# A rewoven order behind convolution 2, and x2 copied as whole rows of 66

## The chip, the core and the metric

The kernel runs on one core of a Trainium2 chip. The metric is device time in microseconds (us), the median of repeated executions; lower is better.

## The reference

Eight images of 64 x 64 pixels and 48 channels, float32, NHWC, go through four layers in a row:

```python
# L0: channel attention (q, k, v from a 48x144 product, gram of q and k over the 4096 pixels),
#     then 1x1 conv 96->96, leaky ReLU, 3x3 conv 96->96, leaky ReLU, 1x1 conv 96->48, plus x
# L1: 3x3 depthwise conv, 1x1 conv 48->48, batch norm, after a ReLU
# L2: router = sigmoid(mean over pixels @ Wr + br), 4 experts;
#     1x1 expand 48->192 (mixed weights), ReLU, 3x3 depthwise (mixed), ReLU, 1x1 48<-192, plus its input
# L3: as L1, other weights
```

Each image's layer 2 needs the mean of layer 1's whole output, and each image's convolution in layer 0 needs sums over all of its pixels; these are the two points at which an image can't go on by chunks.

## The kernel before

Every engine has its instructions written out by hand: one function `iteration(f, attn, back)` for each, with the same meaning of its three images. While image f is in convolution 2, layer 1 and the start of layer 2, image attn = f + 1 is in the attention of layer 0, and image back = f - 1 is in the end of layer 2 and layer 3. Iteration 0 and 7 stand apart (no back, no attn); 1 to 6 are a loop. The rest of image 7 follows behind the loop.

An image is handled in chunks of 512 pixels (one PSUM bank, `BANK`): 8 chunks for layer 0 and the expansion (`CHUNKS`), and, with even and odd rows on separate partitions (0 to 47, and 64 to 111), 4 chunks in layers 1 and 3 and in the projection (`PCHUNKS`). PSUM's eight banks are four rings of two (`Ring`); `take` makes PE wait until the reader of the entry two before is done.

PE (line 1261): conv2, 8 chunks of 24 matmuls, then w3 (96->48); l1 and l3 are `pair_conv` (1154 ff.), 15 matmuls a chunk, 5 of them on `b_parts`, shifted copies that SyncE makes by six DMAs a chunk (`copy_beside`, 876 and 880), once the high and low parts of this chunk and the next are there. transpose_x, attention_scores, attention_sums (1078), attention_gather and attention_weights are the attention of attn; project (1230 ff.) and out_tokens (1245) belong to back; routing, expand_halo and expand (1181 f.) to f. conv1 weaves q transposes (1105), conv1's matmuls (1113) and the expansions.

ScalarE (line 1472): it takes PSUM out: x_out (1330), scores_out, two squares a group (1340), l1_out (1434 with an accumulator, then 1438), project_affine (1425, 1426), l3_out (1448), tokens_out (1461), the sigmoid of route (1443) and the square roots; first_tap and finish_unit (1386) belong to the depthwise units.

VectorE (line 794): the depthwise taps (659, 1024 elements a partition each; `steps_at` says how many stand in which place, the last four numbers after convolution 2), low parts (`l1_low_part`, `l3_low_part`, line 738: v minus its high part; `x2_low_part`, 751), mean_out (756, 758), norms_begin (594 to 602: it waits for all 16 squares of attn, releases `u_ready` at 596, and goes on to the norms of q), mix_weights (767 to 791), norms_end (609 to 612), the sums' copies (620 to 624), conv1_weights (629 to 633), and the h1b rows of the expansion (667, 675).

GpSimd: scale_k (997) after `u_ready`, which PE's attention_sums waits for, and the low parts of conv1's output.

SyncE's queue, in this order: load of x, `beside_l1` (4 times `copy_beside`), `beside_l3` (4 times), `copy_x2` (903), the store of back (912), `copy_thirds`. The layer 1 result is written as x2_h and x2_l into rows 33 to 64 of `y1_parts`, columns 1 to 64 of 66; copy_x2 brings it to `x2`, where expansion and project read it: four DMAs, each 48 partitions of 32 rows of 64 numbers, once project of back is done with the old x2.

## Time and profile before

| | |
|---|---|
| median of 3 runs | 1163.04 us (1160.52 to 1165.03) |
| the profiled execution | 1161.86 us, its span 1160.0 us |
| PE busy | 1049.4 us, 4808 matmuls |
| VectorE busy | 858.6 us |
| ScalarE busy | 470.9 us |
| GpSimd busy | 90.4 us |
| granted TensorE clock, mean | 0.963 |

The profile is of one execution. The busy times of engines overlap. A busy PE is one whose matmuls are in flight; a clock of 1.00 is 2.4 GHz, 0.50 is 1.2 GHz. In the timeline a row merges neighbouring instructions of one line; the brackets behind it give the idle time of the engine ahead of it and what released it.

### The profile page before, as it was taken

To read this page: it belongs to the slowest core of one execution; us is meant where nothing else is said; L and a number is where in the kernel's file an instruction comes from. 1 tells how busy PE (TensorE), PEld (TensorE's weight loads), DVE (VectorE), ACT (ScalarE), POOL (GpSimd) and SP (SyncE) were. 2 spreads that over 40 slices of the span, in tenths; PEclk is the share of its full clock that TensorE was granted. 3 is DMA by queue.
4 is the path that set the end of the run, shared out by engine and by line. 5 is a ranking of instruction groups with operands and counts; after the bars stand their busy time and mean duration, and the time that the engine had idled before them with its cause. 6 is when DMAs were issued, how large, how long until landed. Compare 5 with 4: busy or idle time off the path is not lost.

```text
span 1160.0 us, 14937 instructions
## 1 busy us (share of the span) xinstructions
PE 1049.4 (90%) x4808; PEld 667.8 (58%) x4808; DVE 858.6 (74%) x1193; ACT 470.9 (41%) x812; POOL 90.4 (8%) x72
## 2 busy tenths in 40 slices
PE   4699789998999999999999999999999999977986
PEld 3465566556665666556665666557565666535534
DVE  6742569976798669976899659976799669972870
ACT  3311533354533643354533633354523643334331
POOL 0300011000200011000200011000200011000000
PEclk9889979999999999999999989999999999989998
DMA  4224325236423545236523535236423551236114
GB/s 67 60 53 73 73 39 88 48 77 127 91 32 72 112 85 87 45 76 125 101 33 80 109 73 87 45 72 124 94 34 79 111 87 43 47 71 131 21 24 97
DMA packets 169904, 86.79 MB, mean 75 GB/s; under 512 B 145455, under 2 KB 146324, under 8 KB 169876
## 3 DMA queue, kind: packets, MB, share of 16 engines
q1 hardware_dynamic: 169876, 86.44, 40.1%
q8 instruction: 15, 0.25, 0.1%
q14 instruction: 13, 0.11, 0.0%
HBM read 10.82 MB, written 6.29 MB: 15 GB/s over the span
## 4 chain that ended last, share of the span: by engine, by line
PE 63%; DVE 13%; issue 9%; SPq 6%; ACT 4%; DMA 4%; POOL 0%; DVEq 0%; ACTq 0%; POOLq 0%
PE bank L1132 12%; PE bank L1137 12%; PE bank L1143 8%; DVE dwa L659 6%; PE bank L1166 5%; PE bank L1113 4%; PE bank L1234 4%; DMA x_odd<-y_parts 3%; PE bank L1154 3%; PE bank L1181 3%; SPq L903 2%; PE bank L1182 2%; PE bank L1105 2%; SPq L876 2%; PE bank L1169 2%
## 5 line engine op out<-in xcount | busy, mean ns | idle before, releaser
L659 DVE SCALAR_TENSOR_TENSOR dwa<-h1a,dyn,dwa 128x1024 f32<-128x1024 f32 x240 | 293.2, 1276 | 0.0
L659 DVE SCALAR_TENSOR_TENSOR dwb<-h1b,dyn,dwb 128x1024 f32<-128x1024 f32 x128 | 155.9, 1275 | 0.0
L1132 PE MATMUL bank<-y_parts,w_l 96*96 96x512 f32 x576 | 152.1, 409 | 0.0
L1137 PE MATMUL bank<-y_parts,w_h 128*96 128x512 f32 x576 | 148.7, 402 | 0.0
L1166 PE MATMUL bank<-a_parts,wt_h 128*112 128x512 f32 x384 | 118.2, 416 | 11.8 <-ACT dwa L1448 7.7
L1132 PEld LDWEIGHTS bank<-y_parts,w_l 96*96 96x96 f32 x576 | 91.7, 163 | 61.0 <-issue 21.3
L1137 PEld LDWEIGHTS bank<-y_parts,w_h 128*96 128x96 f32 x576 | 93.8, 163 | 44.6
L1166 PEld LDWEIGHTS bank<-a_parts,wt_h 128*112 128x112 f32 x384 | 64.1, 177 | 46.0 <-issue 16.9
L1003 POOL TENSOR_TENSOR y_parts<-y,y_parts 96x512 fp32r<-96x512 f32 x56 | 67.1, 1199 | 203.6 <-DVE y L699 203.5
L1398 ACT ACTIVATE y<-bank,b2s 96x512 f32<-96x512 f32 x32 | 21.9, 683 | 141.2 <-PE bank L1143 141.2
L1143 PE MATMUL bank<-y_parts,w_one 128*96 128x512 f32 x192 | 76.6, 399 | 0.0
L1143 PE MATMUL bank<-y_parts,w_two 128*96 128x512 f32 x192 | 76.2, 397 | 0.0
L738 DVE SCALAR_TENSOR_TENSOR a_parts<-v,a_parts 112x512 fp32r<-112x512 f32 x64 | 43.5, 689 | 43.2 <-ACT a_parts L1426 40.4
L997 POOL TENSOR_TENSOR tok<-tok,u 128x1536 f32<-128x1536 f32 x8 | 22.4, 2796 | 667.2 <-DVE u L596 667.2
L1113 PE MATMUL bank<-xq,w_cur 97*96 97x512 f32 x128 | 66.8, 603 | 3.5 <-DVE y L699 3.5
L1398 ACT ACTIVATE xq<-bank,b2s 96x512 f32<-96x512 f32 x32 | 21.9, 685 | 117.0 <-PE bank L1143 108.4
L698 DVE TENSOR_TENSOR y_parts<-bank,y 96x512 fp32r<-96x512 f32 x64 | 44.0, 687 | 22.8 <-ACT y L1370 22.7
L1448 ACT ACTIVATE dwa<-bank,conv_bias,inv 112x512 f32<-112x512 f32 x32 | 24.9, 778 | 83.5 <-PE bank L1169 83.5
L1166 PE MATMUL bank<-a_parts,wt_l 128*112 128x512 f32 x192 | 57.0, 405 | 0.0
L1068 PE MATMUL bank<-qkw,xcm 113*128 113x192 f32 x256 | 49.6, 337 | 7.1 <-ACT tok L1340 5.3
L1363 ACT ACTIVATE xq<-bank 96x512 f32<-96x512 f32 x64 | 37.5, 586 | 41.6 <-PE bank L1105 41.6
L1168 PE MATMUL bank<-y_parts,wt_h 128*112 128x512 f32 x128 | 51.3, 401 | 0.0
(246 smaller groups left out, 1706.9 us busy)
## 6 DMA issues: line engine op xcount, KB each, us to landing
y_parts<-a_parts SPq DMA_DIRECT2D x64, 198.0 KB, 3.0
y_parts<-a_parts SPq DMA_DIRECT2D x64, 197.6 KB, 3.4
tok<-in_x_dram SPq DMA_DIRECT2D x48, 192.0 KB, 4.8
a_parts<-a_parts SPq DMA_DIRECT2D x128, 66.0 KB, 2.4
y_parts<-y_parts SPq DMA_DIRECT2D x64, 131.9 KB, 2.3
x_even<-y_parts SPq DMA_DIRECT2D x16, 384.0 KB, 7.5
x_odd<-y_parts SPq DMA_DIRECT2D x16, 384.0 KB, 9.9
out_dram<-dwb SPq DMA_DIRECT2D x32, 192.0 KB, 4.1
```

What stands on the lines that cost most here:

```text
L659: nc.vector.scalar_tensor_tensor(out=dst, in0=tap_input(n, t), scalar=weight, in1=dst, op0=ALU.mult, op1=ALU.add).then_inc(tap_step, 1)
L698: nc.vector.tensor_tensor(y1_view(y1_h, k - 1), bank.rearrange("p (j w) -> p j w", w=W), y1_tokens(k - 1), ALU.max).then_inc(y1h_ready, 1)
L1003: nc.gpsimd.tensor_tensor(y1_view(y1_l, k), y1_tokens(k), y1_view(y1_h, k).bitcast(F32), ALU.subtract).then_inc(y1l_ready, 1)
L1068: last = nc.tensor.matmul(bank[:, m * 2 * C2:(m + 1) * 2 * C2], xcm[:, i * 128:(i + 1) * 128], qkw[:, :], start=True, stop=True)
L1113: nc.tensor.matmul(bank[0:C2, :], w1_cur[:, :], xq[:, (k - 1) % 2, :], start=True, stop=True)\
L1132: nc.tensor.matmul(bank[0:C2, :], w2_l[:, t, :], y1_h[:, rows, cols], start=t == 0, stop=False)
L1137: nc.tensor.matmul(bank[0:C2, :], w2_h[:, t, :], y1_parts[:, 0, rows, cols], start=False, stop=False)
L1143: last = nc.tensor.matmul(bank[0:C2, :], wgt[:, kh, :], y1_parts[:, 1, rows, cols], start=False, stop=kh == 2 and kw == 2)
L1166: nc.tensor.matmul(bank[0:P2, :], wgt[layer][:, kw, :], own[:, rows, kw:kw + W], start=n + kw == 0, stop=False)
L1168: nc.tensor.matmul(bank[0:P2, :], wgt[layer][:, 3, :], beside[:, rows, 1:W + 1], start=False, stop=False)
L1234: last = nc.tensor.matmul(bank[par * ODD_AT:par * ODD_AT + C, :], pc[:, part, :], src[:, :, par, :], start=False, stop=n == 1)
L1398: nc.scalar.activation(y2[(k // 2) % 2][:, (k % 2) * BANK:(k % 2 + 1) * BANK], ring_c.bank(C_2 + k)[0:C2, :], ACT.Identity, bias=b2s[:, 0: ...
```

## The change

PE's order behind convolution 2 becomes: l1(0), w3(3), x transposes, project(0, 1), l1(1), transposes, scores 0 to 3, l1(2), scores 4 to 7, project(2), l1(3), project(3), routing, l3(0), half of the attention sums, l3(1), out_tokens(0), the other half, l3(2), out_tokens(1), gather, l3(3), weights, out_tokens(2), halo, out_tokens(3), expand 0 and 1, and conv1. ScalarE's and VectorE's orders follow it: norms_begin is cut in two, its first part (to `u_ready`) goes between x2_low_part(1) and (2), its second behind mix_weights; l3_low_part(3) goes behind route. `gs` lies in the tile `routed` now, as do the mixed expansion weights before it. `x2` has rows of 66 and is copied in two halves of four DMAs, each 48 partitions of one contiguous run (16 rows of 66); half 0 goes ahead of chunk 1 of `beside_l3`. Expansion and project read columns 1 to 64 of x2's rows. Of VectorE's taps behind convolution 2 one moves from before l3_low_part(1) to after it.

```diff
--- before.py
+++ after.py
@@ -60,7 +60,7 @@
-B_COPIES, WT_COPIES, X2_COPIES = 6, 24, 4
+B_COPIES, WT_COPIES, X2_COPIES = 6, 24, 8
 THIRD = C2 // 3
@@ -163,14 +163,14 @@
         s1, s2, u, r = (sb(n, [128, k, 2 * RUN]) for n, k in (("s1", 2), ("s2", 1), ("u", 2), ("r", 1)))
-        gs, twin = sb("gs", [P2, SUMS]), sb("twin", [P2, C])
+        twin = sb("twin", [P2, C])
         gt, gm = sb("gt", [SUMS, C]), sb("gm", [SUMS, C])
...
         routed = sb("routed", [P2, M])
-        wk, mean_b = routed[0:C2, :], routed[:, 0:128]
+        wk, mean_b, gs = routed[0:C2, :], routed[:, 0:128], routed[:, 0:SUMS]
         ew_h, ew_l = (sb(n, [C2, E_ALL], F32R) for n in ("ew_h", "ew_l"))
@@ -195,7 +195,7 @@
-        x2 = [sb(f"x2_{name}", [C2, HALF], F32R) for name in ("even", "odd")]
+        x2 = [sb(f"x2_{name}", [C2, PAIRS, WP], F32R) for name in ("even", "odd")]
@@ -432,9 +432,7 @@
         POOL_CHUNKS = CHUNKS - 1
-        EARLY_SCORES = 4
-        BEFORE = -1
-        expand_beside = {BEFORE: (0, 1), 7: (), 8: (9, 10, 11), **{k: (k + 2,) for k in range(7)}}
+        expand_beside = {7: (), 8: (9, 10, 11), **{k: (k + 2,) for k in range(7)}}
@@ -612,21 +613,30 @@
-            def sums_out(image):
+            def sums_apart(image):
...
+            def sums_out(image):
+                bank = ring_a.bank(A_G)
                 both_parities = bank[0:SUMS, 128:128 + C]
...
-            def conv1_weights(image):
+            def norm_of_k(image):
...
+            def conv1_weights(image):
+                bank = ring_a.bank(A_M2)
                 dve.wait_ge(root_k, image + 1)
@@ -798,29 +806,37 @@
                 if back is not None:
+                    depthwise_at(back, BY_PROJECT + 2)
                     l3_low_part(back, 0)
-                    depthwise_at(back, BY_PROJECT + 2)
                     l3_low_part(back, 1)
...
                 x2_low_part(f, 0)
+                x2_low_part(f, 1)
+                if attn is not None:
+                    norms_begin(attn)
+                x2_low_part(f, 2)
                 if back is not None:
                     l3_low_part(back, 2)
-                x2_low_part(f, 1)
-                if back is not None:
-                    l3_low_part(back, 3)
-                x2_low_part(f, 2)
                 mean_out(f)
...
                 route(f)
-                if attn is not None:
-                    norms_begin(attn)
+                if back is not None:
+                    l3_low_part(back, 3)
                 mix_weights(f)
                 if attn is not None:
+                    norms_of_q(attn)
+                    sums_apart(attn)
                     norms_end(attn)
                     sums_out(attn)
+                halo_out(f)
+                if attn is not None:
+                    norm_of_k(attn)
+                h1b_rows(f, 0)
+                if attn is not None:
                     conv1_weights(attn)
+                h1b_rows(f, 1)
                 conv1_out(attn, f)
@@ -893,15 +912,19 @@
-        def copy_x2(sp, f):
-
-            wait(sp, x2h_ready, PCHUNKS * f + PCHUNKS)
-            wait(sp, x2l_ready, PCHUNKS * f + PCHUNKS)
-            wait(sp, project_done, 2 * PCHUNKS * f)
+        def copy_x2(sp, f, half):
+            chunks = PCHUNKS // 2 * (half + 1)
+            wait(sp, x2h_ready, PCHUNKS * f + chunks)
+            wait(sp, x2l_ready, PCHUNKS * f + chunks)
+            wait(sp, project_done, 2 * (PCHUNKS * (f - 1) + chunks))
+            rows = slice(half * PAIRS // 2, (half + 1) * PAIRS // 2)
             for par in range(2):
-                for n, src in enumerate((x2_h, x2_l)):
-                    sp.dma_start(x2[par][n * C:(n + 1) * C, :].bitcast(F32).rearrange("p (j w) -> p j w", w=W),
-                                 src[par * ODD_AT:par * ODD_AT + C, :, :].bitcast(F32)).then_inc(x2_copied, 16)
+                for part in range(2):
+                    dst = x2[par][part * C:(part + 1) * C, rows, :]
+                    src = y1_parts[par * ODD_AT:par * ODD_AT + C, part, PAIRS + 1 + rows.start:PAIRS + 1 + rows.stop, :]
+                    dst, src = (t.bitcast(F32).rearrange("p h w -> p (h w)") for t in (dst, src))
+                    sp.dma_start(dst, src).then_inc(x2_copied, 16)
@@ -920,8 +943,8 @@
-        def beside_l3(sp, b, l1_images):
-            for m in range(PCHUNKS):
+        def beside_l3(sp, b, l1_images, quarters=range(PCHUNKS)):
+            for m in quarters:
                 wait(sp, l1_done, PCHUNKS * l1_images - 3 + m)
@@ -964,8 +987,11 @@
                 if back is not None:
-                    beside_l3(sp, back, f + 1)
-                copy_x2(sp, f)
+                    beside_l3(sp, back, f + 1, (0,))
+                copy_x2(sp, f, 0)
+                if back is not None:
+                    beside_l3(sp, back, f + 1, range(1, PCHUNKS))
+                copy_x2(sp, f, 1)
                 if back is not None:
@@ -1069,11 +1095,13 @@
-            def attention_sums(image):
-
-                bank = ring_a.take(pe, image, A_G)
-                pe.wait_ge(k_scaled, image + 1)
-                for i in range(RUN):
+            def attention_sums(image, runs):
+                bank = ring_a.bank(A_G)
+                if runs.start == 0:
+                    ring_a.take(pe, image, A_G)
+                    pe.wait_ge(k_scaled, image + 1)
+                for i in runs:
                     for par, at in enumerate((0, ODD_AT)):
@@ -1177,7 +1205,7 @@
-                src = x2[par][:, rows.start * W:rows.stop * W]
+                src = x2[par][:, rows, 1:W + 1]
                 nc.tensor.matmul(out_ap, ew_h[:, at:at + M1], src, start=start, stop=False)
@@ -1226,9 +1254,9 @@
                     other = dwb[:, :, :].rearrange("p (j b) w -> p j b w", b=2)[:, m2 * ROWS:(m2 + 1) * ROWS]
-                    pixels = slice(m * BANK, (m + 1) * BANK)
-                    nc.tensor.matmul(bank[0:P2, :], pick[:, :], x2[1][:, pixels], start=True, stop=False)
-                    nc.tensor.matmul(bank[0:C, :], pick[:, ODD_AT:P2], x2[0][:, pixels], start=False, stop=False)
+                    rows = slice(m * ROWS, (m + 1) * ROWS)
+                    nc.tensor.matmul(bank[0:P2, :], pick[:, :], x2[1][:, rows, 1:W + 1], start=True, stop=False)
+                    nc.tensor.matmul(bank[0:C, :], pick[:, ODD_AT:P2], x2[0][:, rows, 1:W + 1], start=False, stop=False)
                     for n, (part, src) in enumerate(((0, first), (1 + m // 2, other))):
@@ -1260,12 +1288,7 @@
                 conv2(f)
-                if back is not None:
-                    project(back, (0,))
-                w3(f, PCHUNKS - 1)
-                if back is not None:
-                    project(back, (1,))
-                else:
+                if back is None:
                     pe.wait_ge(prep_dve, marks["pairs"])
@@ -1273,35 +1296,55 @@
                                          start=True, stop=True).then_inc(prep_pe, 1)
-                for m in range(2):
-                    l1(f, (m,))
-                    if attn is not None:
-                        transpose_x(attn, (2 * m, 2 * m + 1))
-                if attn is not None:
-                    attention_scores(attn, range(EARLY_SCORES))
+                l1(f, (0,))
+                w3(f, PCHUNKS - 1)
+                if attn is not None:
+                    transpose_x(attn, (0, 1))
+                if back is not None:
+                    project(back, (0, 1))
+                l1(f, (1,))
+                if attn is not None:
+                    transpose_x(attn, (2, 3))
+                    attention_scores(attn, range(4))
                 l1(f, (2,))
-                if back is not None:
-                    project(back, (2, 3))
+                if attn is not None:
+                    attention_scores(attn, range(4, 8))
+                if back is not None:
+                    project(back, (2,))
                 l1(f, (3,))
-                if attn is not None:
-                    attention_scores(attn, range(EARLY_SCORES, 8))
+                if back is not None:
+                    project(back, (3,))
                 routing(f)
                 if back is not None:
-                    l3_and_out(back)
-                if attn is not None:
-                    attention_sums(attn)
-                if back is not None:
-                    out_tokens(back, (PCHUNKS - 1,))
+                    l3(back, (0,))
+                if attn is not None:
+                    attention_sums(attn, range(RUN // 2))
+                if back is not None:
+                    l3(back, (1,))
+                    out_tokens(back, (0,))
+                if attn is not None:
+                    attention_sums(attn, range(RUN // 2, RUN))
+                if back is not None:
+                    l3(back, (2,))
+                    out_tokens(back, (1,))
                 if attn is not None:
                     attention_gather(attn)
+                if back is not None:
+                    l3(back, (3,))
+                if attn is not None:
+                    attention_weights(attn)
+                if back is not None:
+                    out_tokens(back, (2,))
                 expand_halo(f)
-                if attn is not None:
-                    attention_weights(attn)
+                if back is not None:
+                    out_tokens(back, (3,))
+                expand(f, 0)
+                expand(f, 1)
                 conv1(attn, f)
...
             attention_scores(0, range(8))
-            attention_sums(0)
+            attention_sums(0, range(RUN))
             attention_gather(0)
@@ -1471,31 +1514,31 @@
                 conv2_slope(f, back)
-                if back is not None:
-                    project_affine(back, f + 1, 0)
                 l1_high_part(f, PCHUNKS - 1)
-                if back is not None:
-                    project_affine(back, f + 1, 1)
                 if attn is not None:
...
                 l1_out(f, (0,))
+                if back is not None:
+                    project_affine(back, f + 1, 0)
+                    project_affine(back, f + 1, 1)
                 if attn is not None:
                     x_out(attn, (2, 3))
-                if attn is not None:
-                    scores_out(attn, range(2))
+                    scores_out(attn, range(4))
                 l1_out(f, (1,))
                 if attn is not None:
-                    scores_out(attn, range(2, EARLY_SCORES))
+                    scores_out(attn, (4, 5))
                 if back is not None:
                     finish_unit(back, 4)
+                if attn is not None:
+                    scores_out(attn, (6, 7))
+                if back is not None:
                     finish_unit(back, 5)
...
                     project_affine(back, f + 1, 2)
+                l1_out(f, (3,))
+                if back is not None:
                     project_affine(back, f + 1, 3)
-                l1_out(f, (3,))
-                if attn is not None:
-                    scores_out(attn, range(EARLY_SCORES, 8))
                 route(f)
```

Left out: the same cuts in the functions themselves (sums_out, conv1_weights and norms_begin cut in two, the first step of the loop over k taken out of conv1 and its partners), and the calls for image 0 ahead of the loop.

## Rows read from the trace of the kernel before

**Rows 1.** The page's part 1: busy us, share of the span, instructions.

```profile
PE 1049.4 (90%) x4808; PEld 667.8 (58%) x4808; DVE 858.6 (74%) x1193; ACT 470.9 (41%) x812; POOL 90.4 (8%) x72
```

**Rows 2.** PE timeline where convolution 2 starts: start us, us, line, operation, tiles, count.

```profile
179.18 2.29 PE L1132 MATMUL bank<-y_parts,w_l 96*96 96x512 f32 x9
...
832.93 2.38 PE L1132 MATMUL bank<-y_parts,w_l 96*96 96x512 f32 x9
...
961.84 2.31 PE L1132 MATMUL bank<-y_parts,w_l 96*96 96x512 f32 x9
```

**Rows 3.** Granted clock, image 5: window, us, PE busy, clock, DMA share, GB/s.

```profile
754.00:756.00 2.00, 2.00 (x8) 0.59 0.11 26
```

**Rows 4.** PE timeline, image 5 behind convolution 2; brackets: idle before, its releaser.

```profile
753.01 0.49 PE L1230 MATMUL bank<-x_odd,pick 96*112 96x512 f32 x1 [1.72 <-ACT dwa L1386]
...
760.57 0.97 PE L1166 MATMUL bank<-a_parts,wt_h 128*112 128x512 f32 x3
...
764.23 1.03 PE L1057 MATMUL bank<-ident,tok 128*112 128x128 f32 x8
...
769.93 3.13 PE L1068 MATMUL bank<-qkw,xcm 113*128 113x192 f32 x16 [0.25 <-ACT xcm L1330]
...
777.47 0.49 PE L1230 MATMUL bank<-x_odd,pick 96*112 96x512 f32 x1 [0.84 <-ACT dwa L1386]
...
788.36 1.57 PE L1068 MATMUL bank<-qkw,xcm 113*128 113x192 f32 x8 [0.76 <-ACT tok L1340]
...
798.13 0.97 PE L1166 MATMUL bank<-a_parts,wt_h 128*112 128x512 f32 x3 [0.48 <-ACT dwa L1448]
...
806.97 2.88 PE L1078 MATMUL bank<-tok 128*48 128x97 f32 x64
...
811.30 0.30 PE L1181 MATMUL bank<-x_even,ew_h 96*128 96x64 f32 x1 [0.41 <-DMA x_odd<-y_parts]
...
814.39 0.51 PE L1181 MATMUL bank<-x_odd,ew_h 96*128 96x512 f32 x1 [0.98 <-DVE h1b L667]
...
815.43 0.60 PE L1105 MATMUL bank<-ident,tok 128*96 128x128 f32 x4
```

**Rows 5.** Timeline of VectorE (DVE) and GpSimd (POOL), same image.

```profile
758.22 0.75 DVE L728 SCALAR_TENSOR_TENSOR v<-bank,col,xcm 112x512 f32<-112x512 f32 x1 [4.23 <-PE bank L1154]
...
790.55 3.35 DVE L594 TENSOR_REDUCE s<-tok 128x64 f32<-128x3072 f32 x1 [0.31 <-ACT tok L1340]
...
794.80 2.80 POOL L997 TENSOR_TENSOR tok<-tok,u 128x1536 f32<-128x1536 f32 x1 [93.04 <-DVE u L596]
...
796.61 1.04 DVE L600 TENSOR_TENSOR s<-s,u 128x32 f32<-128x32 f32 x1
797.68 0.19 DVE L601 TENSOR_TENSOR s<-s,u 128x32 f32<-128x32 f32 x1
```

**Rows 6.** Timeline of ScalarE (ACT), same image.

```profile
770.89 1.20 ACT L1340 ACTIVATE tok<-bank 128x192 f32<-128x192 f32 x4 [0.52 <-PE bank L1068]
...
776.36 2.25 ACT L1386 ACTIVATE dwa<-dwa 128x1024 f32<-128x1024 f32 x2 [1.96 <-DVE dwa L659]
```

**Rows 7.** SyncE's DMA issues, same image, then the DMA issues by size with us to landing.

```profile
795.39 2.62 SPq L903 DMA_DIRECT2D x_even<-y_parts  x2
798.06 7.31 SPq L903 DMA_DIRECT2D x_odd<-y_parts  x2
...
y_parts<-y_parts SPq DMA_DIRECT2D x64, 131.9 KB, 2.3
```

**Rows 8.** Timeline of PE and DVE in the last iteration, image 7.

```profile
1072.93 0.39 PE L1181 MATMUL bank<-x_even,ew_h 96*128 96x64 f32 x1 [3.33 <-issue]
...
1080.83 1.53 DVE L655 TENSOR_SCALAR dwb<-h1b,dyn 128x1024 f32<-128x1024 f32 x2
```

**Rows 9.** Timeline of DVE and PE at the very end, layer 3 of image 7.

```profile
1124.14 0.69 DVE L738 SCALAR_TENSOR_TENSOR a_parts<-v,a_parts 112x512 fp32r<-112x512 f32 x1 [0.46 <-ACT a_parts L1426]
...
1132.09 0.93 PE L1166 MATMUL bank<-a_parts,wt_h 128*112 128x512 f32 x3 [4.08 <-DMA y_parts<-a_parts]
```

More of the change, by code:

```diff
@@ L304, in conv_chain_kernel @@
         BY_CONV1, BY_CONV2, BY_PROJECT = 0, CHUNKS, 2 * CHUNKS
-        steps_at = (0,) * CHUNKS + (7, 4, 4, 4, 4, 4, 4, 4) + (1, 1, 6, 7)
+        steps_at = (0,) * CHUNKS + (7, 4, 4, 4, 4, 4, 4, 4) + (1, 1, 5, 8)
         assert sum(steps_at) == TAP_STEPS
@@ L596, in norms_begin, with norms_of_q @@
                 nc.vector.reciprocal(u[:, :, :], s1[:, :, :]).then_inc(u_ready, 1)
+            def norms_of_q(image):
                 dve.wait_ge(q4_ready, image + 1)
@@ L686, in conv1_out @@
                     nc.vector.memset(y1_parts[APART:128, :, 1:H + 1, 0:WP:WP - 1].bitcast(F32), 0.0).then_inc(edge_cleared, 1)
-                if f is not None:
-                    halo_out(f)
-                for k in range(BEFORE, CHUNKS + 1):
+                for k in range(CHUNKS + 1):
                     for n in expand_beside[k] if f is not None else ():
@@ L830, in _ @@
             norms_begin(0)
+            norms_of_q(0)
             norms_end(0)
+            sums_apart(0)
             sums_out(0)
+            norm_of_k(0)
             conv1_weights(0)
@@ L1095, in conv1 @@
             def conv1(image, f):
-                for k in range(BEFORE, CHUNKS + 1):
-                    if image is not None and 0 <= k < CHUNKS:
+                for k in range(CHUNKS + 1):
+                    if image is not None and k < CHUNKS:
                         if k == 0:
@@ L1355, in conv1_slope @@
             def conv1_slope(image, f):
-                for k in range(BEFORE, CHUNKS + 1):
-                    if image is not None and 0 <= k < CHUNKS:
+                for k in range(CHUNKS + 1):
+                    if image is not None and k < CHUNKS:
                         act.wait_ge(xqt_done, CHUNKS * image + k + 1)
@@ L1508, in iteration @@
                     l3_and_tokens_out(back, (2, 3))
-                    tokens_out(back, (PCHUNKS - 1,))
                 if attn is not None:
                     root_of_k(attn)
+                if back is not None:
+                    tokens_out(back, (PCHUNKS - 1,))
                 act.wait_ge(weight_chain.sem, weight_chain.each * (f + 1))
```

2 lines of the change are left out of this document (1 added, 1 removed).

## The prediction

> **What bounds the kernel now.** I read the page's busy shares first: PE, the tensor engine, is busy 90% of the span [rows 1], so only its idle time, its clock and the two ends are to be won. The timeline then gives the loop's period: convolution 2 of image 1 starts at 179.18, of image 7 at 961.84 [rows 2], six periods of 130.44 us. The last of them, from 832.93, takes 128.91; it is one in which no row shows a lowered clock. In others the granted clock falls to half for some us (0.59 over 754 to 756 [rows 3], just behind an idle 1.72), and the mean says that this costs 1.5 us a period.
>
> The PE timeline of image 5 [rows 4] shows where PE stands still between convolution 2 and the first q transpose (815.43): 1.72 before project(0), 0.25 before the first scores, 0.84 before project(2), 0.76 in the late scores, 0.48 twice between layer 3's chunks (one row stands for both), 0.41 at the halo, 0.98 before expansion 1. That is 5.9 us; the undisturbed period has the same but for the 0.41. Behind 815.43, conv1 and expansions run to 832.93 at PE's own pace, and the change leaves them alone.
>
> **The change, step by step.** All times are in image 5's frame, PE's steps at full clock. Convolution 2 ends at 751.15 (753.01 less its wait and dispatch). Layer 1's chunk is 764.23 - 760.57 = 3.66, a pair of x transposes 0.79, two groups of scores 1.42, the sums over 64 products 2.81 [rows 4]; a projection costs 2.5, w3 1.0.
>
> Layer 1 chunk 0 goes first. Its copies were asked for during convolution 2, so it starts at once and covers the outputs of convolution 2 that w3(3) waits for, and later the Relu that project(0) waited for. PE: l1(0) 754.8, w3(3) 755.8, transposes 756.6, projects 0 and 1 761.6, l1(1) 765.3, transposes 766.1, wait 0.5 (ScalarE's x_out; it was 0.25), scores 0-3 769.4, l1(2) 773.0, scores 4-7 with 0.1 of waits 775.95. The 1.72 is gone, and the 0.76, since no l1_out now stands between the scores on ScalarE.
>
> Project(2) waits for unit 4 of the depthwise taps. VectorE idled 4.23 before w3_out at 758.22 [rows 5], and ScalarE could finish unit 4 at 776.36 [rows 6], with only taps and low parts between; w3(3) done 2.1 earlier gives unit 4 at 774.2 and the last tap at 775.3. ScalarE must first square scores 4 and 5 (1.20 for two groups), then finish the unit (2.25 for two) [rows 6], so project(2) starts at 776.4: 0.45 idle for 0.84. Then l1(3) to 782.6, project(3) 785.1.
>
> Moved on VectorE: norms_begin now stands ahead of x2_low(2), l3_low(2), mean_out and route. It waits for the squares of group 7 (777.5 on ScalarE) and takes 790.55 to 794.72, 4.2 us [rows 5]; VectorE's queue behind it is held until 781.8. At that moment GpSimd's scale_k is released, 2.80 us long. **Here is the dear step.** In before, L600, 32 elements a partition with two SBUF inputs, started beside scale_k at 796.61 and ended with it, 1.04 us; its twin L601 behind it took 0.19 [rows 5]. The tensor_reduce with one input beside scale_k was not longer. So an operation with two SBUF inputs waits until GpSimd is done. x2_low(2) can slip in ahead (0.7), GpSimd then runs 782.4 to 785.2, and l3_low(2), two inputs too, ends at 785.9 instead of 783.0. mean_out behind it ends 786.3, routing waits 1.3 us for it.
>
> The Trainium skill says the same as a rule (SBUF — State Buffer, section SBUF: two separate sides): the pair shared by VectorE and GpSimd is an exclusive lock for the whole instruction, taken by whichever starts first. This trace's 1.04 against 0.19 agrees; by it x2_low(2) goes first, and who is next is not said.
>
> l3_low(2) also releases the copies of layer 3's chunk 1. At the end of the kernel a low part begun at 1124.14 (0.69) let the matmul go at 1132.09 [rows 9]: 7.26 us from its end for six copies. So l3(1) can't start before 793.2; PE, with l3(0) and half the sums behind routing, is there at 791.6: 1.6 idle. Price of the collision: 2.9 us a period. x2_low(3), rwz and the sigmoid still end near 788.1, as the table load (ScalarE, behind project_affine(3)) hides them; mix_weights (5.3) ends at 793.5, norms_of_q (2.4 without the lock), the sums' copies and norms_end fit behind l3(2), as the other half of the sums and a transpose now stand between layer 3's chunks and cover the two 0.48.
>
> SyncE: half 0 of x2 is asked for at 776.8, ahead of layer 3's chunk 1, in four issues. The latter are not due before 783, and 2.5 to 5 us of issuing are over by then: no cost. Half 1 follows chunk 3's copies. Before, four copies of 384 KB in rows of 256 bytes took 811.30 - 795.39 = 15.9 us from first issue to the halo [rows 7, 4]. The copies now are 198 KB, 48 contiguous runs; the nearest row is 131.9 KB in 2.3 us [rows 7], the dearest x2's own. I take 3 us each, by bytes from the nearest, with issues at 0.6 to 1.3 (2.62 for two [rows 7]): half 1, asked for from 797.8, has landed at 803 to 806, against a halo at 807.7 (with the collision). Cost nothing, 2 to 5 of cover; at the old price it becomes the bound (below). The matmuls on x2 read rows with a stride of 66, as those on y1_parts do: priced at nothing, 0.03 us a matmul (some 0.9 a period) at worst.
>
> At the end of the stage out_tokens(3) hides the halo's output and expansion 0 follows, so the 0.98 goes. Without the collision the q transposes start at 807.7, where an undisturbed period had them at 832.93 + 111.4 (17.5 before the next convolution 2), or 813.2 in this frame: 5.5 us saved, and 2.6 with it.
>
> **Clock.** Dips were behind idle stretches; 1.3 + 1.6 near each other are as large as the old 1.72. I keep half, 0.7 a period. So the period becomes 126.3 + 0.7 = 127.0, 3.4 x 6 = 20.6 us less.
>
> **Ends.** Image 0: x, scores and norms come some 6 us earlier, but norms_of_q now stands behind mix_weights and routing behind norms_begin; by the same counting the weights of conv1 are ready 1.7 us earlier (0 to 4). Image 7 has no attention: the halo waited until 1072.93, and the last taps started at 1080.83 [rows 8]. Project(2), bound there by the taps, gains 2.1 with w3(3), routing gets project(3) as its cover, and x2's copies no longer hold up the halo, at about 1064. The taps need the store before them to have landed: issued some 1065 to 1069, landed 1072.3. They start 8.5 us earlier (4 to 9), and from there VectorE sets the end as before.
>
> **Sum.** The profiled execution is 1161.86 us with a span of 1160.0; 1161.9 - 20.6 - 1.7 - 8.5 = 1131.1. The median of before is 1.2 above that execution, so I forecast 1132.
>
> **Rivals.**
> A. VectorE keeps the port. Its next operation starts some 0.08 before the last one ends, so l3_low(2) may also go ahead of GpSimd; then only x2_low(3), which has room, meets it. 5.5 + 1.3 of clock a period is 41 us, with the ends (10.2) 1111. For it: nothing shows who comes next. Against: GpSimd's request is older. 0.27.
> B. Idle time comes back somewhere else or the clock falls behind both new waits as it did at its longest (2.9 in a period): steady gain 1 us a period and less at the end, 1148. For it: ScalarE's order is new and each of its waits lies in PE's path. 0.12.
> C. The dips come twice in each period and eat the gain; or the copies gain nothing else than their cover: no change, 1160. 0.05.
> D. Slower: the cost of a copy of x2 isn't in its row length, and there are twice as many. Half 0 at the old price keeps SyncE issuing from 776.8 to 786.7 (795.39 to 805.37 before [rows 7]), 0.8 past l3_low(2); chunk 3's copies end 0.8 later, at 798.6; four copies at 15.9 put the halo at 814.5 instead of 811.3, and with halo, transposes and two expansions (2.9) behind it the q transposes at 817.4, 2.0 later than now: 12 us in six periods, less 2 at the ends, 1173. It decides from the point at which half 1 lands later than 807.7 + 3. For it: twice as many copies; against: the 2.3 us row. 0.06.
> That the weave isn't what runs is hardly to be had: each engine's order is written out.
>
> **Chances.** The forecast case has 0.50. The range takes in A and B: 1108 to 1150. The measurement can tell some 0.5%, or 6 us: faster 0.89, same 0.05, slower 0.06.
>
> **What would show it.** Right: no idle before project(0), period near 127; l3_low(2) or x2_low(2) three us long beside scale_k; idle of about 1.3 before routing and 1.6 before l3(1). With A these are gone, period near 124. x2's copies landing in about 3 us, halo waiting for no DMA; last taps before 1075 less what the loop saved. Wrong: a halo waiting for DMA (D), or project(2) waiting over 1 us, ScalarE being the new bound.

## The result, and the profile after

The kernel after takes 1117.54 us (median of 4 runs, 1116.46 to 1120.20) against 1163.8 for before on the same chip: a ratio of 0.961, 95% interval 0.958 to 0.964. The forecast was 1132 with a range of 1108 to 1150. The sign and most of the steps held; the gain was 15 us larger than the sum, and the time lies between the forecast's case and rival A's. The profiled execution takes 1118.24 us, its span is 1116.4.

First the page's part 1 (busy us, share of the span, instructions). PE has lost 14 us of busy time against [rows 1] with the same 4808 matmuls, which is what a higher clock looks like there:

```profile
PE 1035.4 (93%) x4808; PEld 658.5 (59%) x4808; DVE 867.4 (78%) x1193; ACT 468.9 (42%) x812; POOL 92.6 (8%) x72
```

PE's timeline where convolution 2 starts, the rows that answer to [rows 2] (start us, us, line, operation, tiles, count):

```profile
174.11 1.12 PE L1160 MATMUL bank<-y_parts,w_l 96*96 96x512 f32 x4
...
800.58 1.67 PE L1160 MATMUL bank<-y_parts,w_l 96*96 96x512 f32 x6
...
925.80 0.88 PE L1160 MATMUL bank<-y_parts,w_l 96*96 96x512 f32 x3
```

Six periods take 925.80 - 174.11 = 751.69, 125.28 each, and all six lie between 125.17 and 125.43. Those of before had a mean of 130.44. A dip is here a stretch in which the granted clock is at 1.2 GHz. The gain of 43.6 us between the two profiled executions splits like this:

| stretch | before | after | gain | predicted |
|---|---|---|---|---|
| start of the span to the first convolution 2 | 59.39 | 58.13 | 1.3 | 0 |
| from there to convolution 2 of image 1 | 119.79 | 115.98 | 3.8 | 1.7 |
| six periods | 782.66 | 751.69 | 31.0 | 20.6 |
| convolution 2 of image 7 to the end | 198.16 | 190.60 | 7.6 | 8.5 |

The first row is not the change's: the same prologue took between 58.1 and 61.0 in the executions below. Each row compares one execution with one, and the dips ahead of image 7's halo fell differently in the two (13.7 us in before, 6.8 in after), which is part of the last row's 7.6.

The granted clock of the first and the last period of the loop (window, us, PE busy, clock, DMA share, GB/s), against 0.97 to 1.00 in the periods of before and the dip of [rows 3]; no period in between is below 1.00:

```profile
174.10:299.50 125.40, 122.45 (x589) 1.00 0.43 86
...
800.60:925.80 125.20, 122.23 (x589) 1.00 0.43 84
```

PE's timeline of image 5, to be laid beside [rows 4]. Convolution 2 ends at 724.66, so 26.49 is to be added for the frame of the prediction:

```profile
724.66 0.87 PE L1194 MATMUL bank<-a_parts,wt_h 128*112 128x512 f32 x3
...
728.32 1.08 PE L1182 MATMUL bank<-y,w3p 96*64 96x512 f32 x4
...
740.14 3.13 PE L1094 MATMUL bank<-qkw,xcm 113*128 113x192 f32 x16 [0.25 <-ACT xcm L1373]
...
749.75 0.49 PE L1258 MATMUL bank<-x_odd,pick 96*112 96x512 f32 x1
...
759.07 0.36 PE L1203 MATMUL bank<-wr,routed 112*128 112x4 f32 x2 [0.66 <-DVE routed L766]
...
765.42 0.94 PE L1194 MATMUL bank<-a_parts,wt_h 128*112 128x512 f32 x3 [0.84 <-DMA y_parts<-a_parts]
...
775.65 0.97 PE L1194 MATMUL bank<-a_parts,wt_h 128*112 128x512 f32 x3 [0.35 <-ACT dwa L1491]
...
779.40 0.37 PE L1120 MATMUL bank<-wva_aug,gt 97*48 97x96 f32 x2
...
780.12 0.28 PE L1209 MATMUL bank<-x_even,ew_h 96*128 96x64 f32 x1
...
782.93 0.60 PE L1133 MATMUL bank<-ident,tok 128*96 128x128 f32 x4
```

Between convolution 2 and the first q transpose (782.93) the idle is 0.25 + 0.66 + 0.84 + 0.35 = 2.10; in an undisturbed period of before it was 5.5 [rows 4]. That is 3.4 of the 128.91 - 125.28 = 3.6 between an undisturbed period of before and one of after. The other 1.5 of the 5.2 gained per period is the mean price of the dips, which are gone altogether.

Before had four dips in the loop. Those of images 2 and 5 came behind the 1.72. That of image 4 began after 0.41 at the halo, and that of image 1 after the 0.98 ahead of expansion 1, both in images in which the 1.72 drew none. Image 1 of before, the wait and then the clock (windows as above):

```profile
289.83 0.56 PE L1181 MATMUL bank<-x_odd,ew_h 96*128 96x512 f32 x1 [0.98 <-DVE h1b L667]
```

```profile
290.00:292.00 2.00, 2.00 (x7) 0.53 0.90 162
```

VectorE and GpSimd of the same image, which answer to [rows 5]:

```profile
750.62 3.35 DVE L592 TENSOR_REDUCE s<-tok 128x64 f32<-128x3072 f32 x1 [0.64 <-ACT tok L1383]
...
754.70 0.63 DVE L759 TENSOR_TENSOR y_parts<-y,y_parts 112x512 fp32r<-112x512 f32 x1
755.25 3.28 DVE L746 SCALAR_TENSOR_TENSOR a_parts<-v,a_parts 112x512 fp32r<-112x512 f32 x1
```

```profile
754.86 3.12 POOL L1023 TENSOR_TENSOR tok<-tok,u 128x1536 f32<-128x1536 f32 x1 [79.51 <-DVE u L594]
```

The collision is there as it was drawn: x2_low(2) goes first, scale_k (3.12 now, 2.80 in [rows 5]) begins while it runs, and l3_low(2) (L746) takes 3.28 instead of 0.69, to 758.53. It is so in all six periods (3.28 to 3.29). mean_out and routing follow it, and so does the copy that l3(1) waits for.

x2's copies, part 6 of the page (count, KB each, median us to landing); before had 384 KB in 7.5 and 9.9:

```profile
x_even<-y_parts SPq DMA_DIRECT2D x32, 198.0 KB, 3.6
x_odd<-y_parts SPq DMA_DIRECT2D x32, 198.0 KB, 4.0
```

The last iteration, against [rows 8]. PE and then VectorE:

```profile
999.19 0.74 PE L1258 MATMUL bank<-x_odd,pick 96*112 96x512 f32 x1 [6.17 <-ACT dwa L1429]
...
1027.79 0.28 PE L1209 MATMUL bank<-x_even,ew_h 96*128 96x64 f32 x1
```

```profile
1036.48 1.53 DVE L665 TENSOR_SCALAR dwb<-h1b,dyn 128x1024 f32<-128x1024 f32 x2 [2.52 <-DMA out_dram<-dwb]
```

The halo no longer waits (3.33 before), and the last taps start 110.7 behind convolution 2 of image 7 instead of 119.0, bound by the store.

### The profile page after: what moved, and what is told of

Its sections match the earlier page's. It is cut to its first block, busy times and chain, and to the rows that moved or that the text cites. A ratio compares the mean times of both kernels' runs of the same rounds, so it can differ in the third digit from the quotient of the medians.

```text
span 1116.4 us, 14998 instructions
## 1 busy us (share of the span) xinstructions
PE 1035.4 (93%) x4808; PEld 658.5 (59%) x4808; DVE 867.4 (78%) x1193; ACT 468.9 (42%) x812; POOL 92.6 (8%) x72
## 4 chain that ended last, share of the span: by engine, by line
PE 66%; DVE 16%; issue 7%; SPq 4%; DMA 3%; ACT 3%; POOL 0%; ACTq 0%; DVEq 0%; POOLq 0%
PE bank L1160 13%; PE bank L1165 12%; PE bank L1171 8%; PE bank L1194 7%; DVE dwa L669 4%; PE bank L1141 4%; PE bank L1262 3%; PE bank L1182 3%; DMA y_parts<-a_parts 3%; DVE a_parts L746 2%; DVE s L592 2%; PE bank L1209 2%; PE bank L1210 2%; PE bank L1197 2%; PE bank L1196 2%
## 5 line engine op out<-in xcount | busy, mean ns | idle before, releaser
L1194 PE MATMUL bank<-a_parts,wt_h 128*112 128x512 f32 x384 | 117.7, 415 | 14.4 <-DMA y_parts<-a_parts 10.8
L746 DVE SCALAR_TENSOR_TENSOR a_parts<-v,a_parts 112x512 fp32r<-112x512 f32 x64 | 59.0, 932 | 16.7 <-ACT a_parts L1469 13.8
L1197 PE MATMUL bank<-y_parts,wt_h 128*112 128x512 f32 x128 | 51.6, 403 | 0.0
L1196 PE MATMUL bank<-y_parts,wt_h 128*112 128x512 f32 x128 | 51.3, 401 | 0.0
```

Of the source, the lines that this page charges most:

```text
L746: return nc.vector.scalar_tensor_tensor(out=lo[:, rows, 1:W + 1], in0=src[:, m % 2, :].rearrange("p (j w) -> p j w", w=W), scalar=0.0, in1 ...
L1194: nc.tensor.matmul(bank[0:P2, :], wgt[layer][:, kw, :], own[:, rows, kw:kw + W], start=n + kw == 0, stop=False)
L1196: nc.tensor.matmul(bank[0:P2, :], wgt[layer][:, 3, :], beside[:, rows, 1:W + 1], start=False, stop=False)
L1197: last = nc.tensor.matmul(bank[0:P2, :], wgt[layer][:, 4, :], beside[:, rows, 2:W + 2], start=False, stop=n == 2)
```

## Experiments

The theory: the order gives the gain, by covering waits and so keeping the clock up; the collision with GpSimd is real and costs the 1.5 a period that the two waits show. Its rivals: the waits before routing and l3(1) have another cause; one part of the order alone gives the gain; or x2's rows give it. Times of different groups are compared by their ratio to the kernel before on the same chip. "Period" is the mean distance from convolution 2 to the next in the loop.

| kernel | us | ratio (95%) | period |
|---|---|---|---|
| before | 1163.8 | 1 | 130.44 |
| after | 1117.54 | 0.961 (0.958 to 0.964) | 125.28 |
| late_scale | 1110.04 | 0.957 (0.954 to 0.960) | 123.65 |
| halved_scale | 1111.81 | 0.959 (0.955 to 0.962) | 124.07 |
| norms_late | 1149.39 | 0.990 (0.987 to 0.994) | 129.91 |
| project0_first | 1133.17 | 0.977 (0.973 to 0.981) | 127.77 |
| sums_whole | 1166.85 | 1.005 (1.002 to 1.008) | 133.27 |
| rows_of_64 | 1117.79 | 0.961 (0.956 to 0.966) | 125.05 |
| one_copy | 1150.12 | 0.989 (0.983 to 0.994) | 129.51 |
| one_copy_rows_of_64 | 1190.77 | 1.027 (1.022 to 1.033) | 135.49 |
| before_rows_of_66 | 1152.43 | 0.992 (0.989 to 0.995) | 130.47 |
| before_l1_first | 1190.76 | 1.023 (1.018 to 1.028) | 135.39 |
| best | 1106.15 | 0.952 (0.948 to 0.956) | 123.63 |
| best_rows_of_64 | 1108.14 | 0.954 (0.950 to 0.957) | 123.62 |

**late_scale: the collision moved away.** scale_k waits until the mean is out.

```diff
             with pool.Fori(1, IMAGES) as image:
+                pool.wait_ge(mean_ready, image)
                 scale_k(image)
```

> The changed kernel, with one wait more: GpSimd's scale_k of image f + 1 waits for mean_ready of image f, so it runs behind l3_low(2) and mean_out instead of beside them. Theory (the port collision): l3_low(2) takes 0.69 us again instead of 3.28, routing and layer 3's chunk 1 lose their idle time (0.66 and 0.84), the period falls from 125.28 by 1.5 to 123.8, the time to about 1108.5 from 1117.5. In image 0 nothing is gained, since mix_weights then meets scale_k. Rival (the wait for routing comes from norms_begin's 4.1 us ahead of mean_out, not from a port): the time stays at 1117, and l3_low(2) stays long or the idle stays.

The period is 1.63 shorter, and both waits (0.66 and 0.84) are gone. VectorE, then GpSimd, in image 5:

```profile
752.63 0.68 DVE L746 SCALAR_TENSOR_TENSOR a_parts<-v,a_parts 112x512 fp32r<-112x512 f32 x1
...
757.27 1.71 DVE L746 SCALAR_TENSOR_TENSOR a_parts<-v,a_parts 112x512 fp32r<-112x512 f32 x1 [0.94 <-ACT a_parts L1470]
```

```profile
755.14 3.29 POOL L1023 TENSOR_TENSOR tok<-tok,u 128x1536 f32<-128x1536 f32 x1 [82.41 <-DVE routed L766]
```

l3_low(2) is short again; now l3_low(3) meets scale_k, and it has room. So the two waits were the collision's, 1.6 us a period. Image 0 loses 1.5 by the later release: its routing waits 2.31 for 4.62, but its sums now wait 2.89 for GpSimd.

**halved_scale: two instructions in place of one.**

```diff
-                nc.gpsimd.tensor_tensor(k, k, columns(u[:, :, :], 2 * RUN, [[1, 2 * RUN], [0, C]]), ALU.mult).then_inc(k_scaled, 1)
+                for b in range(2):
...
-                    pe.wait_ge(k_scaled, image + 1)
+                    pe.wait_ge(k_scaled, 2 * image + 2)
```

> The changed kernel with scale_k as two GpSimd instructions of half the size. If a waiting VectorE operation gets the port at the end of one GpSimd instruction, l3_low(2) ends some 1.5 us earlier, the idle before routing and before layer 3's chunk 1 goes, and the time is near 1108.5; if GpSimd keeps the port from one instruction to the next, or if the port is not the cause, 1117.5.

GpSimd and then VectorE:

```profile
749.80 3.71 POOL L1024 TENSOR_TENSOR tok<-tok,u 128x768 f32<-128x768 f32 x2 [79.51 <-DVE u L594]
```

```profile
750.18 1.98 DVE L746 SCALAR_TENSOR_TENSOR a_parts<-v,a_parts 112x512 fp32r<-112x512 f32 x1
...
752.26 1.33 DVE L766 TENSOR_SCALAR routed<-ones,mean 112x128 f32<-112x128 f32 x1
```

l3_low(2) is let in between the two halves, and the mean's broadcast (L766) then waits for the second: 1.33 for 0.29. Most of the price is back (routing waits 0.38, l3(1) not at all), without a wait added to GpSimd.

**norms_late: norms_begin back behind route.**

```diff
                 x2_low_part(f, 1)
-                if attn is not None:
-                    norms_begin(attn)
                 x2_low_part(f, 2)
...
                 route(f)
+                if attn is not None:
+                    norms_begin(attn)
```

> The changed kernel with norms_begin put back behind route, everything else as changed. Theory: no collision at l3_low(2) (0.69 us, no idle before routing), but k_scaled comes some 12 us later than now, at 4.5 us behind the first half of the sums' turn, and mix_weights behind it, 4 us later: the period grows by 3 to 5 us, 1135 to 1147. Rival (the early norms bring nothing since the sums would be covered): 1108.

The first sums of image 5 wait, and behind that the clock falls (windows as above):

```profile
792.73 1.58 PE L1106 MATMUL bank<-tok 128*48 128x97 f32 x28 [4.13 <-POOL tok L1023]
```

```profile
792.00:794.00 2.00, 1.27 (x28) 0.94 0.73 141
794.00:796.00 2.00, 2.00 (x12) 0.50 0.77 173
796.00:798.00 2.00, 2.00 (x8) 0.71 0.67 136
```

A wait of 4.13 in place of 1.50 makes 2.6 a period; the other 2.0 of the 4.63 lost is the clock. Without the early norms 0.5 of the 5.2 us a period is left of the new order's gain.

**project0_first: layer 1's chunk back behind project(0) and w3(3).**

```diff
-                l1(f, (0,))
+                if back is not None:
+                    project(back, (0,))
                 w3(f, PCHUNKS - 1)
+                l1(f, (0,))
...
-                    project(back, (0, 1))
+                    project(back, (1,))
```

> The changed kernel with project(0) and w3(3) ahead of layer 1's chunk 0, as before the change. The idle of 1.72 us ahead of project(0) is back in six periods and in image 7: at least +1.7 x 7 = 12, so 1129. If that idle is what the lowered clock stretches came from, they are back in some of the periods (0.5 to 1.5 us a period more, 1133 to 1138); if not, the clock stays at 1.00 in the loop and it is 1129.

The wait of [rows 4] is back to the hundredth, and in image 5 the four matmuls behind the first four take 1.92 instead of 1.03:

```profile
738.99 0.49 PE L1258 MATMUL bank<-x_odd,pick 96*112 96x512 f32 x1 [1.72 <-ACT dwa L1431]
739.32 0.41 PE L1259 MATMUL bank<-x_even,pick 96*48 96x512 f32 x1
739.66 1.10 PE L1262 MATMUL bank<-dwa,pc 128*48 128x512 f32 x4
740.55 1.92 PE L1262 MATMUL bank<-dwb,pc 128*48 128x512 f32 x4
```

The periods alternate: 128.50, 127.00, 128.53, 127.00, 128.75, 126.81. The wait of 1.72 costs 1.7 in each, and a dip 1.5 to 1.9 more in every other. The same idle thus draws a dip in one image and none in the next.

**sums_whole: the attention sums in one piece behind layer 3.**

```diff
-                if attn is not None:
-                    attention_sums(attn, range(RUN // 2))
...
-                if attn is not None:
-                    attention_sums(attn, range(RUN // 2, RUN))
...
                     l3(back, (3,))
+                if attn is not None:
+                    attention_sums(attn, range(RUN))
```

> The changed kernel with all 64 products of the attention sums behind layer 3's chunk 3, then out_tokens(2), gather and weights. The two waits for ScalarE (0.48) between layer 3's chunks come back, layer 3's chunk 1 waits 1.4 longer for its copies, and the chain sums, gs, gather, gt, weights stands uncovered with about 1.5 us: period 128 to 129, 1135 to 1140. Rival (the halves only move the work): 1118 to 1122.

The whole gain is gone. PE in image 5, and the clock there:

```profile
800.25 0.94 PE L1194 MATMUL bank<-a_parts,wt_h 128*112 128x512 f32 x3 [2.43 <-DMA y_parts<-a_parts]
...
804.91 0.96 PE L1194 MATMUL bank<-a_parts,wt_h 128*112 128x512 f32 x3 [0.48 <-ACT dwa L1487]
...
819.74 0.53 PE L1120 MATMUL bank<-wva_aug,gt 97*48 97x96 f32 x2 [2.48 <-DVE gm L629]
```

```profile
818.00:820.00 2.00, 0.26 (x2) 0.77 0.00 0
820.00:822.00 2.00, 2.00 (x13) 0.50 0.00 0
822.00:824.00 2.00, 2.00 (x6) 0.50 0.00 0
```

Without the first half l3(1) comes before its copies, 2.43; the second half no longer covers the 0.48 twice; and gather and weights stand close behind the sums, 2.48. That is 4.7 more idle; the rest of the 8.0 a period (3.3) goes with a clock that is at 1.2 GHz behind the 2.48. Here every period has a dip of nearly seven us, and a mean clock of 0.97.

**rows_of_64: halves kept, rows of 64.** x2 is `[C2, PAIRS, W]`, the copies read columns 1 to 64 of each row.

```diff
-                    src = y1_parts[par * ODD_AT:par * ODD_AT + C, part, PAIRS + 1 + rows.start:PAIRS + 1 + rows.stop, :]
+                    src = y1_parts[par * ODD_AT:par * ODD_AT + C, part, PAIRS + 1 + rows.start:PAIRS + 1 + rows.stop, 1:W + 1]
```

> The changed kernel with x2 in rows of 64 again, copied in the same two halves of four DMAs, but in runs of 256 bytes. Theory (a copy's time goes by its number of rows): half 1 has half the rows of the old copy, 8 us instead of 15.9 from its first issue, landed at the halo's turn: 1117 to 1121, and conv1's stage with expansion 17.50 instead of 17.65 us, if the stride of 66 costs anything. Rival (a fixed price for each copy): halo 7.5 us late in each period, 1162.

```profile
x_even<-y_parts SPq DMA_DIRECT2D x32, 192.0 KB, 4.3
x_odd<-y_parts SPq DMA_DIRECT2D x32, 192.0 KB, 5.2
```

The same time as after. The copies are slower and still early enough (the halo waits in image 7 alone, 0.89); in exchange the matmuls that read x2 are spaced 0.235 instead of 0.24, which is 0.2 of the period. The rows of 66 give nothing that the times could show once the copy is halved.

**one_copy and one_copy_rows_of_64: x2 whole behind layer 3's last copies,** with rows of 66 and of 64.

```diff
-            chunks = PCHUNKS // 2 * (half + 1)
+            chunks = PCHUNKS
...
-            rows = slice(half * PAIRS // 2, (half + 1) * PAIRS // 2)
+            rows = slice(0, PAIRS)
...
-                copy_x2(sp, f, 0)
```

> The changed kernel with rows of 66, but x2 copied whole, in four DMAs behind the last copies of layer 3, as before the change. By bytes (3.6 to 4.0 us for 198 KB) 396 KB lands some 8 to 9 us after the first issue, about 0.5 to 1 us behind the halo's turn: 1120 to 1124. Rival (the halves bring nothing): 1117.

> The kernel one_copy with x2 in rows of 64, that is, the old copy at its old place in the new order: runs of 256 bytes, whole, behind layer 3's copies. Landing 15.9 us from its first issue it makes the halo wait 7.5 us a period, against 2.29 with rows of 66, and a lowered clock behind it: period 134 to 135, 1170 to 1176. Rival (halving alone matters, the rows don't): 1150.

The halo of image 5 in the one, and in the other:

```profile
805.96 0.30 PE L1208 MATMUL bank<-x_even,ew_h 96*128 96x64 f32 x1 [2.29 <-DMA x_odd<-y_parts]
```

```profile
833.41 0.42 PE L1208 MATMUL bank<-x_even,ew_h 96*128 96x64 f32 x1 [6.84 <-DMA x_odd<-y_parts]
```

With rows of 66, one period has no dip and takes 127.63, which is 125.28 and the wait; the other five take 129.4 to 131.4. With rows of 64 the first matmul behind the wait already runs at half clock (0.42 for 0.30) and the period is 10.2 longer in the mean: 7.4 of wait (6.84 in image 5), the rest clock. So a whole copy makes the halo wait in either form, and 5 us longer in short rows; a halved one does in neither.

**before_rows_of_66: only the form of the copy, in the old order.** x2 gets its rows of 66 in the kernel before, and `gs` its place in `routed`, for room; the copies stay whole.

> The kernel before, with x2 in rows of 66 and copied in one contiguous run a partition, whole, at its old place (gs in the tile routed, for room). It lands some 7 us earlier, but only 0.41 of idle in some periods and 2 to 3 us in image 7 hang on it: 1158 to 1161. Rival (the rows carry the gain of the change): under 1150.

The period stays (130.47), since only 0.41 waited for the copy there. But the last iteration takes 190.03 instead of 198.16, and its last taps start 7.2 earlier. What they follow has changed. In before no DMA held them: the halo waited 3.33 [rows 8], PE ran the expansions behind it at half clock (1072 to 1079), and VectorE's rows of h1b waited for each of them. In this kernel the halo doesn't wait, and the store is the bound. VectorE of before, then of this kernel:

```profile
1077.57 0.75 DVE L675 TENSOR_SCALAR h1b<-bank,dyn 128x512 f32<-128x512 f32 x1 [0.96 <-PE bank L1182]
```

```profile
1072.11 1.53 DVE L655 TENSOR_SCALAR dwb<-h1b,dyn 128x1024 f32<-128x1024 f32 x2 [1.51 <-DMA out_dram<-dwb]
```

The store is issued 105.5 behind convolution 2 instead of 108.4, and those 2.9 are not the copy's: PE's waits up to there add up to 10.8 and 10.9, but before had 13.7 us of dips on the way in this execution and before_rows_of_66 6.8. So at the end this alone is worth as much as the whole change (8.1 against 7.6), in one execution each and with up to 2.9 of it from where the dips fell. The medians differ by 10.3 us, more than was expected.

**before_l1_first: only layer 1's chunk 0 first, in the old order.**

```diff
                 conv2(f)
+                l1(f, (0,))
                 if back is not None:
                     project(back, (0,))
```

> The kernel before, with layer 1's chunk 0 ahead of project(0) on PE and nothing else. The idle of 1.72 is covered, but w3(3) starts 1.9 later, the taps with it, and project(2), which waits for unit 4, shows 0.84 + 1.72 + 1.9 = 4.5 of idle: period +1.9 or more, 1175. Rival (covering the idle is worth what it is long, wherever it is done): -1.7 and the dips behind it, 1145 to 1153.

```profile
796.90 0.77 PE L1230 MATMUL bank<-x_odd,pick 96*112 96x512 f32 x1 [4.44 <-ACT dwa L1388]
```

Slower than before. PE comes to project(2) 1.72 sooner, since that wait is gone, while w3(3), and with it the taps and unit 4, come 1.9 later (3.66 less 1.72): 0.84 + 1.72 + 1.94 = 4.5, and 4.44 is what it waits. Only 1.9 of the 4.95 us that the period grows is idle time. The rest goes with the clock: it is at 1.2 GHz for nearly seven us around this wait, and every period has a second dip at the 0.98 ahead of expansion 1, where before had one in six periods.

**best and best_rows_of_64: both remedies.** scale_k of the loop waits for the mean from image 2 on, and in the last iteration, where no scores stand between, l1(3) goes ahead of project(2).

```diff
-            with pool.Fori(1, IMAGES) as image:
+            scale_k(1)
+            split_y1(1)
+            with pool.Fori(2, IMAGES) as image:
+                pool.wait_ge(mean_ready, image)
...
+                if attn is None:
+                    l1(f, (3,))
                 if back is not None:
                     project(back, (2,))
```

> The changed kernel with two edits. GpSimd's scale_k waits for mean_ready of the image before from image 2 on (image 1's runs at once, as in the changed kernel: image 0 has nothing to hide it), which against late_scale should give back 1.5 us in iteration 0. In the last iteration layer 1's chunk 3 goes ahead of project(2), which stood idle for 6.2 us there: 3.5 us less. Period 123.65 as in late_scale, 1105 in all. If the last iteration is bound further on (the store ahead of the last taps), the second edit brings nothing: 1108.5.

> The kernel best with x2 in rows of 64, copied in halves. If the stride of 66 costs conv1's stage 0.15 to 0.2 us a period and the halves land in time, 1.0 to 1.4 less than best: 1105, which is at the edge of what a comparison can tell; the period should read 123.4 to 123.5. If the copies come late behind layer 3's, 1108 or more.

PE of best in the last iteration, project(2) and the l3 chunk whose copies are now late:

```profile
991.66 0.46 PE L1261 MATMUL bank<-x_odd,pick 96*112 96x512 f32 x1 [1.61 <-ACT dwa L1435]
...
1004.39 0.93 PE L1197 MATMUL bank<-a_parts,wt_h 128*112 128x512 f32 x3 [2.09 <-DMA y_parts<-a_parts]
```

The wait of 6.17 shrinks to 1.61, l3 waits 2.09 for 1.04 in return, and the last stretch takes 186.73 instead of 190.60. With the period of 123.63 this has the lowest ratio, 0.952, but its interval overlaps that of late_scale: the two periods are alike, and the gain on it lies in image 0 and the end. With rows of 64 it is the same within the intervals, though the same l3 chunk waits 5.04 there.

## Why the prediction was right, and where its sum fell short

**The order (5.5 a period): right.** Without the collision and without dips the working gives 130.44 - 1.5 - 5.5 = 123.4; late_scale, which has neither, takes 123.65. The 1.72, the late scores' 0.76 and the 0.98 are gone, norms_begin starts at 777.1 in the prediction's frame (said: 777.5), half 1 of x2 is asked for at 798.2 (said: 797.8), and the halo starts at 806.6 (said: 807.7) and waits for nothing. Project(2) was to wait 0.45 and doesn't: PE came 0.3 later than put, and the unit was ready 0.2 sooner.

**The collision (2.9 a period): the mechanism right, the term too large.** It costs 1.5 in waits by the trace of after and 1.63 by late_scale. l3_low(2) ended at 785.0 in the prediction's frame, not at 785.9: norms_begin was 0.4 early, x2_low(2) overlapped the end of the reciprocal by 0.2, and GpSimd and the low part behind it took 0.15 less each. Its copies then let l3(1) go 6.9 behind its end and not 7.26. So l3(1) started 1.3 sooner than put. Rival A, that VectorE keeps the port for l3_low(2), is wrong: L746 takes 3.28.

**The clock (0.7 a period left): the second term that was too large.** Nothing is left. Its two waits were to be near enough to the old 1.72 to draw half the dips; they turned out at 0.66 and 0.84, and no dip came in six periods, while project0_first with its 1.72 has one in every other. The step itself, that a wait's length decides, is not borne out: before and before_l1_first have dips behind 0.98, after has none behind 0.96 (image 3). The working never said that taking away the 0.98 also takes away dips. The two terms are 1.4 + 0.7 = 2.1 of a period of 127.0; the order fell 0.25 short, and what is left is the difference between 1.5 and 1.63. Over six periods this is 10.4 of the 12.9 us by which the sum missed; image 0 is 2.1, the prologue 1.3, the end -0.9.

**Image 0 (1.7): 3.8.** The sums waited 7.69 for GpSimd there and gather 3.60; now routing waits 4.62, gather 3.72 and weights 2.29, but the 1.65 before w3(3) and the 0.76 in the scores are gone too. The working followed only the end of the attention.

**The end (8.5): 7.6, with the right bound and a cause too wide.** The taps wait for the store (2.52), start 8.3 earlier and the end follows, as drawn. Project(2) starts 2.4 sooner (said: 2.1) and still waits 6.17. But the new order isn't needed for it: before_rows_of_66 takes 8.1 less with the old one, since what held the taps in before was the halo's wait and the clock behind it (and 2.9 of the 8.1 is where earlier dips fell). The working took the difference of two rows, and so has that clock in it without naming it.

**Rivals B, C and D** are out: no idle left in the loop reaches 1 us, there is no dip, and copies of 198 KB land in about 4 where D needed the old price. D's mechanism is real at another size: with the copy whole, in rows of 64, the halo is the bound and the kernel is slower than before by 2.7%.

**The expectations that missed** missed mostly on one term, the clock behind a wait, which was not counted, or at half of its price: sums_whole, before_l1_first and one_copy_rows_of_64 had their waits near what was put down. In one_copy the wait itself was too small as well (0.5 to 1 put down, 2.3 to 3.2 measured; its four copies had landed 11 us behind the first issue, not 8 to 9). norms_late came out 2 us above its range: its period grew as said, but image 0, which grew by 4.8, was left out. before_rows_of_66 gained 10 us where 2 to 5 were put down, for the reasons given there.

Open: what decides whether one idle of 1.0 to 2.5 is followed by a dip and the next is not. In one_copy 2.50 in image 4 was and 2.29 in image 5 wasn't, in project0_first image 5's 1.72 was and image 6's wasn't. In image 0 of after the collision falls on the mean's broadcast; what it costs there wasn't measured by itself. And the moves that take away the 0.98 ahead of expansion 1 were not run alone.

## What to carry to other kernels

Where PE is 90% busy, price a wait in its list at its length and at the clock that it may cost (here 1.7 us of idle cost 1.5 to 3.5). The parts of one weave don't add up: layer 1 first alone made the kernel slower, and the halved sums or the early norms taken out alone gave back most of the gain or all of it. Keep a long GpSimd instruction on SBUF away from the VectorE operations that someone waits for, by a later release or in shorter pieces, and ask when a copy is needed before making it faster.

## What the runs showed of the hardware

**The port between VectorE and GpSimd.** An operation with one SBUF tensor waits too. In image 0 of after the broadcast of the mean, fp32 from `ones` by a per-partition scalar, takes 2.62 beside scale_k, against a median of 0.286. VectorE and GpSimd:

```profile
136.26 2.62 DVE L766 TENSOR_SCALAR routed<-ones,mean 112x128 f32<-112x128 f32 x1
```

```profile
135.69 3.10 POOL L1023 TENSOR_TENSOR tok<-tok,u 128x1536 f32<-128x1536 f32 x1 [79.12 <-DVE u L594]
```

The Trainium skill (SBUF — State Buffer, section SBUF: two separate sides) names as takers of the pair operations with two SBUF inputs and those in a 2-port mode; the 2.62 agrees if this one runs in such a mode, which no run here shows by itself. The prediction looked at operations with two inputs alone. Who goes next was open, and the runs say: the one that waits, at the end of an instruction. GpSimd got the pair behind x2_low(2) though VectorE had its next operation ready, and VectorE got it between the two halves of halved_scale.

**Row length of a copy within SBUF.** 192 KB in rows of 256 bytes land in 4.3 and 5.2, 198 KB in contiguous runs in 3.6 and 4.0; whole, 7.5 and 9.9 against 6.0 and 7.7 (before and before_rows_of_66). The Trainium skill (DMA: Bandwidth & Descriptors, section Why small descriptors are slow) says that transfers from SBUF to SBUF don't suffer from small pieces. These rows differ from it by about a quarter, and the measurement decides.

**The clock.** PE's clock fell to 1.2 GHz behind idles of 0.98 (image 1 of before, every period of before_l1_first) and of 1.72, in some images and not in others, while 0.96 in image 3 of after drew nothing. A dip of three to four us cost 1.5 to 2 us of the period (project0_first, one_copy, norms_late), one of nearly seven 2 to 3.3 (norms_late, one_copy, sums_whole).
